# First cross attention of a two-layer Perceiver stack: query projection from half-precision parts

## The reference

```
Q = Sq @ Wq_w.T + Wq_b              # Sq = layernorm(x): 4 x 256 tokens, 256 -> 1024 (16 heads of 64)
K = Sk @ Wq_w.T + Wq_b              # Sk = Sv = context: 4 x 4096 rows
V = Sv @ Wq_w.T + Wq_b
qk = einsum('bqd,bkd->bqk', Q1, K1) / sqrt(64)
X1 = softmax(einsum('bqk,bkd->bqd', qk, V1), axis=-1)    # softmax over the 64 features of a head
x = x + X @ out_w.T + out_b
```

## Time and profile before

| | |
|---|---|
| Median of 3 runs | 1931.04 us (1930.85 to 1933.86) |
| Profiled execution | 1943.5 us, span 1941.8 us |
| Mean granted TensorE clock | 0.921 |
| PE busy | 1676.4 us, 86% of the span |
| DVE busy | 1316.1 us, 68% |
| ACT busy | 1083.6 us, 56% |
| Query projection, L1025 | 27.63 us, 64 records |

### The profile page before, as it was taken

The page is one execution under the profiler, slowest core; times in us unless marked ns, Lnnn a source line. Parts: engine busy times, 40 slices in busy tenths (PEclk is TensorE's granted clock), DMA queues, the critical chain, the costliest instruction groups (busy, mean ns, idle before and its releaser), DMA issues.

```text
span 1941.8 us, 34714 instructions
## 1 busy us (share of the span) xinstructions
PE 1676.4 (86%) x13900; PEld 913.9 (47%) x13900; DVE 1316.1 (68%) x2014; ACT 1083.6 (56%) x1942; POOL 276.1 (14%) x248
## 2 busy tenths in 40 slices
PE   6988868999798999846999999999999679886877
PEld 4556645666566888521333333333333433462252
DVE  4223343381276888659999999999991686427867
ACT  3312112888643888311999999999999106311620
POOL 3223001898320000300000000000000000000000
PEclk9989989999888999875999999999999779886978
DMA  8123110899723766266433533543400070118100
GB/s 321 66 87 94 32 44 20 279 282 298 228 96 107 240 237 200 69 100 93 84 60 74 99 65 63 91 84 60 83 25 2 19 98 3 44 35 106 39 1 22
DMA packets 144653, 196.62 MB, mean 101 GB/s; under 512 B 34454, under 2 KB 109864, under 8 KB 140232
## 3 DMA queue, kind: packets, MB, share of 16 engines
q1 hardware_dynamic: 142764, 190.07, 38.1%
q0 software_dynamic: 1728, 4.33, 0.7%
HBM read 143.04 MB, written 51.00 MB: 100 GB/s over the span
## 4 chain that ended last, share of the span: by engine, by line
PE 43%; DVE 41%; issue 5%; POOL 4%; DMA 3%; ACT 2%; SPq 1%; another core or an unknown queue 1%; DVEq 0%; ACTq 0%; POOLq 0%
DVE mx_part L2200 28%; PE bank L1192 5%; PE pair L1234 5%; DVE mx L2309 3%; POOL k_part L2541 2%; PE bank L1045 2%; PE bank L1336 2%; PE pair L1395 2%; PE bank L252 2%; PE pair L1160 2%; PE pair L1147 2%; PE bank L1089 2%; DMA xT<-x_slots 2%; POOL c_lo L2528 2%; PE pair L1551 2%
## 5 line engine op out<-in xcount | busy, mean ns | idle before, releaser
L1743 ACT ACTIVATE pexp_all<-bank 128x512 f32<-128x512 f32 x1024 | 551.9, 595 | 97.9 <-PE bank L1350 84.5
L2200 DVE TENSOR_REDUCE mx_part<-pair 128x2 f32<-128x1024 f32 x512 | 583.0, 1213 | 16.6 <-PE pair L1322 14.2
L1336 PE MATMUL bank<-pexp_all,vst 128*17 128x256 f32 x4096 | 321.4, 386 | 6.0 <-issue 6.0
L1322 PE MATMUL pair<-kst,qs 49*128 49x512 f16 x1024 | 210.0, 407 | 44.7 <-DVE mx_part L2200 28.0
L1350 PE MATMUL bank<-qs,kst 52*128 52x256 f16 x2048 | 203.2, 271 | 0.0
L1322 PEld LDWEIGHTS pair<-kst,qs 49*128 49x128 f16 x1024 | 50.4, 93 | 273.2 <-DVE mx_part L2200 215.0
L1350 PEld LDWEIGHTS bank<-qs,kst 52*128 52x128 f16 x2048 | 120.7, 95 | 57.0 <-ACT pexp_all L1743 18.4
L1760 ACT ACTIVATE pexp_all<-bank 128x512 f32<-128x512 f32 x128 | 67.6, 595 | 120.5 <-PE bank L1458 120.3
L1336 PEld LDWEIGHTS bank<-pexp_all,vst 128*17 128x17 f32 x4096 | 68.6, 95 | 114.7 <-issue 105.3
L1677 ACT ACTIVATE hid_f<-bank,b 128x256 f32<-128x256 f32 (+1 forms) x152 | 78.6, 519 | 51.1 <-PE bank L1192 36.0
L1234 PE MATMUL pair<-w_hi,hid_hi 128*128 128x256 f16 x368 | 101.1, 275 | 3.2 <-issue 1.8
(11 more groups left out here) (323 smaller groups left out, 3042.5 us busy)
## 6 DMA issues: line engine op xcount, KB each, us to landing
w_f<-in_w_all SPq DMA_DIRECT2D x34, 1024.0 KB, 6.2
kst<-k_scr SPq DMA_DIRECT2D x192, 128.0 KB
v_scr<-v_st SPq DMA_DIRECT2D x64, 272.0 KB, 3.3
vst<-v_scr SPq DMA_DIRECT2D x16, 1088.0 KB, 5.6
ctx_sb<-in_ctx SPq DMA_DIRECT2D x16, 1024.0 KB, 5.0
cT<-in_ctxT SPq DMA_DIRECT2D x32, 512.0 KB, 5.6
k_scr<-k_part SPq DMA_DIRECT2D x128, 128.0 KB, 3.6
x_slots<-zeros SPq DMA_DIRECT2D x1, 3840.0 KB, 21.1
```

The costliest lines, as they stand in the source:

```text
L1322: last = pe.matmul(pair[n % 2][:, e * 512:(e + 1) * 512], qs[g % NBK][rws, p, qt * P:(qt + 1) * P], kst[g % NBK][rws, p, kb * 512:(kb + 1) ...
L1336: last = pe.matmul(bank[3][32 * h:32 * h + HV, 0:S], vst[g % 2][:, c, h * HV:(h + 1) * HV], unit_exp[n % NUE][:, p * S:(p + 1) * S], start ...
L1743: act.activation(unit_exp[n % NUE], bank[SCORE_BANKS[n % 3]], ACT.Exp, scale=SCALE).then_inc(s_exp, 1)
L2200: dve.tensor_reduce(mx_part[:, :, 2 * p + qt, kb], pair[n % 2][:, :].rearrange("p (e k) -> p e k", e=2), X_AXIS, ALU.max).then_inc(s_mx, 1)
```

## The change

The projection L1025 is computed from half-precision parts. The scaled weights are split in high and low part, w0q_part, in the memory of tok; the turned tokens likewise, x0_part, in the memory of gw. The high part of the tokens is a second destination of the turn, so ACT copies each tile twice. Each single-precision matmul becomes three with half-precision operands. ACT makes the weights' high parts ahead of the turn, and waits for s_wa there. DVE makes the low parts, of the weights first and then of the tokens, behind the second Gram copy; the addition of the output bias to x moves behind them. PE waits for the count of low parts (s_q0p) in place of the turn. The eviction divides by W_SCALE.

```diff
+            w0q_part = tok[:, :, :].rearrange("p t d -> p (t d)").bitcast(F16).rearrange("p (i k n) -> p i k n", i=2, k=KT)
+            x0_part = gw[:, :, :].rearrange("p k n -> p (k n)").bitcast(F16).rearrange("p (i k n) -> p i k n", i=2, k=KT)
...
-        turn0 = Turn(u, [(xT, None, None)])
+        turn0 = Turn(u, [(xT, None, None), (x0_part[:, 0], None, None)])
...
             for half in range(2):
-                turned(pe, turn0, half)
+                pe.wait_ge(s_q0p, 4 + KT * (half + 1))
                 for m in range(W0 // P):
                     if job >= 2:
                         pe.wait_ge(s_q0e, job - 1)
                     for k in range(KT):
-                        last = pe.matmul(bank[2 + job % 2], w0q[:, k, m * P:(m + 1) * P],
-                                         xT[:, k, half * 512:(half + 1) * 512], start=(k == 0), stop=(k == KT - 1))
+                        for i, (w_, x_) in enumerate(((0, 0), (0, 1), (1, 0))):
+                            last = pe.matmul(bank[2 + job % 2], w0q_part[:, w_, k, m * P:(m + 1) * P],
+                                             x0_part[:, x_, k, half * 512:(half + 1) * 512],
+                                             start=(k == 0 and i == 0), stop=(k == KT - 1 and i == 2))
...
             act.wait_ge(s_start, 16 * N_START)
+            act.wait_ge(s_wa, 32)
+            for i in range(4):
+                k, ns = i // 2, slice(i % 2 * 512, (i % 2 + 1) * 512)
+                act.activation(w0q_part[:, 0, k, ns], w0q[:, k, ns], ACT.Copy, scale=W_SCALE).then_inc(s_q0h, 1)
             act_turn(act, turn0)
...
-                               bias=col("L0_xattn_Wq_b", m)).then_inc(s_q0e, 1)
+                               bias=col("L0_xattn_Wq_b", m), scale=1.0 / W_SCALE).then_inc(s_q0e, 1)
...
                 if b == 0:
                     dve.wait_ge(s_start, 16 * N_START)
-                    st.link(dve.tensor_tensor(x[:, :, :], x[:, :, :], per_tile_rows("L0_xattn_out_b"), ALU.add))
-                    st.settle()
...
                 dve.wait_ge(s_grame, 4 * (b + 1))
+                if b == 0:
+                    for i in range(4):
+                        k, ns = i // 2, slice(i % 2 * 512, (i % 2 + 1) * 512)
+                        dve.wait_ge(s_q0h, i + 1)
+                        dve.scalar_tensor_tensor(out=w0q_part[:, 1, k, ns], in0=w0q[:, k, ns], scalar=W_SCALE,
+                                                 in1=w0q_part[:, 0, k, ns], op0=ALU.mult, op1=ALU.subtract).then_inc(s_q0p, 1)
+                    for half in range(2):
+                        hs = slice(half * 512, (half + 1) * 512)
+                        for k in range(KT):
+                            dve.wait_ge(s_tev, turn0.ev + 2 * (2 * half + k + 1))
+                            dve.tensor_tensor(x0_part[:, 1, k, hs], xT[:, k, hs], x0_part[:, 0, k, hs], ALU.subtract)\
+                                .then_inc(s_q0p, 1)
+                    st.link(dve.tensor_tensor(x[:, :, :], x[:, :, :], per_tile_rows("L0_xattn_out_b"), ALU.add))
+                    st.settle()
```

More of the change, by code:

```diff
@@ L348, in build @@
         s_q0 = sem("q0_product")
+        s_q0h = sem("q0_weights_high")
+        s_q0p = sem("q0_operand_parts")
         s_q0e = sem("q0_copied")
```

## The result

| | before | after |
|---|---|---|
| Median of 5 runs | 1931.77 us (1930.85 to 1933.86) | 1913.98 us (1908.35 to 1919.23) |
| Profiled execution | 1943.5 us, span 1941.8 | 1914.0 us, span 1912.2 |
| Mean granted clock in it | 0.921 | 0.922 |
| Start of the gw products (L1842, after: L1864) | 67.10 | 60.94 |

The ratio is 0.9906, with an interval of 0.9888 to 0.9923: 17.8 us faster by the medians, where 7.1 was forecast.

The account below looks back on a forecast made before the run. The prediction took PE's matmul stream alone to bound the projection (L1025): 6.7 us from the shorter stream plus 0.4 from an earlier start made 7.1, so 1931.0 - 7.1 = 1923.9 us, range 1919 to 1930.

Parts of the forecast that it names:

- Length of the product: Projection L1025: 96 half-precision matmuls at 0.216 us take 20.9 us against 27.6, 6.7 us less.
- Second Gram copy and turn: Ahead of the projection: with the bias add moved, the copy starts at 31.85 and PE turns tokens 1.8 us earlier.
- ACT's conversions hidden behind w0o's arrival: Ahead of the turn: ACT's four weight conversions end at 32.1 to 32.7, hidden with 0.4 to 1.0 us slack.
- third rival: Weight w0o lands 1 to 3 us later, giving 1925 to 1927; chance within a shared 0.16.
- Start of the product: Projection starts at about 36.1 against 36.52 before, a gain taken as 0.4 us.
- Moved add hidden: On DVE behind the low parts: the bias add runs 38.1 to 40.4, hidden; in the open it would cost 2.2 us.
- Evictions: In the projection: ACT's eviction of 0.69 us fits within each 1.30 us job, with 0.5 us to spare.
- fourth rival: In the projection: half-precision matmuls overlap further, ACT's evictions become the bound at 11.0 us, time 1914; chance 0.01.
- All of it should shift together: Behind the projection: later stages keep their length, so the 7.1 us passes whole to the end.
- clock stretches: Behind the edit: a half-clock stretch comes or goes, 4 to 8 us either way; going away, 1915 to 1920, chance 0.09.
- Slower by the clock: Projection at 1.2 GHz takes 41 us, 14 more than before, so about 1944; slower by over 3.9 us has chance 0.06.

Follow-up runs that it names:

- e3: The kernel before with only the output bias addition to x moved behind the second Gram copy; 1926.91 us, ratio 0.9973.
- e7: The changed kernel with only the high-by-high product in the projection, both products with low parts left out; 1913.32 us, ratio 0.9905 to the kernel before.
- e5: The changed kernel again, unchanged, for the scatter of its median and a second profile; 1918.69 us, ratio 0.9935 to the kernel before.
- v1: The changed kernel with the product of Gram matrix and w0q also made from half-precision parts, split on DVE; 1940.75 us, ratio 0.994 to the kernel before.
- c4: The changed kernel with the Gram product from half-precision parts as well, ended after the first cross attention; median 279.34 us.

## Why the prediction was wrong, point by point

- **Length of the product:** forecast 20.9 us, measured 21.68, with 0.8 of it from half clock at its start, and 20.88 in the four other profiles of the changed code, at full clock; 0.216 us per matmul at full clock as in the earlier trace rows. The Trainium skill's sustained spacing of 131 ns (TensorE: Matmul & The Clock Gate, section Back-to-back issue gap) is not seen in this stream; its other formula, 216 ns, agrees with the row. Right.
- **Second Gram copy and turn:** 31.85 forecast, 32.00 measured. e3 gives 1.6 us for this part alone at a like clock in the turn (2.5 against the mean of before), where the prediction had 1.8. Right.
- **ACT's conversions hidden behind w0o's arrival:** end at 32.08, forecast 32.1 to 32.7. The third rival (w0o late) falls.
- **Start of the product:** 36.1 forecast, 36.31 measured. Right; but the start it was compared with, 36.52, was the exception. Five other executions of that code had 37.3 to 37.8, with half clock in the turn, so the gain at this step was nearer 1.3 than 0.4 in most executions.
- **Moved add hidden:** yes, 38.17 to 40.45, wanted at 60.94.
- **Evictions:** ACT idles 0.61 us in each job. The fourth rival falls, though the number that it gave, 1914, is the measured one, by luck. A right number doesn't make a mechanism right: its sign, PE waiting for ACT, is in e7 alone.
- **All of it should shift together:** this is the step that failed. 7.1 us is what the edit saves (7.0 at a like clock, 67.10 to about 60.1), and the prediction took that as the sum for the whole kernel, with the clock stretches at nothing in the sum, as luck in both directions, and a gain from them at 0.09. The runs show three terms more, all on the side of the gain: 1 us from half clock in the turn, which the base has in five of six profiles and the changed code in one of five; 1.3 us from the long stretch, five of six against three of five; and 3.7 us behind the first block, whose length isn't fixed as was assumed "for the rest of the span" but has three levels. The base was one profile, which was the exception in the turn. It had the long stretch at 131.8 in plain sight, with 8.6 us of lost work, and from one profile it couldn't be known whether that was rule or luck. Another 4.6 us of the 17.8 are likely the draw of five executions. What sets how often the stretches come, and which stage makes the levels, stays open.
- **Slower by the clock:** the projection ran at 0.96 mean clock; this rival falls.

The Trainium skill puts such falls of the clock down to PE waiting for DMA between short stages (TensorE: Matmul & The Clock Gate, section HAM oscillation — how this bites in real kernels). In e5's stretch the DMA share is 0.00 and PE is busy 16.14 of 17.1 us, and in the 11.9 us before it, with a DMA share of 0.76, PE was busy for 11.13, as it was in the execution in which the clock stayed full. So no such wait stands ahead of this fall. In v1 PE did wait 6.2 us ahead of its half clock, for DVE and not for a DMA.

No version ran that beats the changed kernel with the whole computation in it: v1 lost what its shorter stream had won in the split on DVE beside POOL. A v1 with that split in another place or on another engine wasn't tried.

## What to carry to other kernels

Splitting a single-precision product into three half-precision ones saves a quarter of its stream when the parts can be made under idle engines; work out which engine makes each part and when its operand lands, and the local saving comes out within a microsecond. Check beside what each of these instructions will run: one that takes 0.4 us alone can take 4.0 beside another engine. Stretches behind the edit, at half clock or not, needn't keep their length when they are reached earlier, so profile the base several times before you call one of its stretches fixed, and compare executions at a like mean clock. A difference of two profiles is no measure: here it was 29.6 us where the medians gave 13 to 18 and the start behind the edited stage 8.

## What was not expected of the hardware

- PE can be granted 1.2 GHz for 17.1 us while busy for 16.1 of them; the same code in another execution gets 3.4 us of it.
- DVE's subtraction of 128x257 took 4.04 us in each of four cases beside POOL's subtraction of ctx_lo (v1, c4), and 0.43 in each of eight without it; the conversion ahead of it 1.37 and 0.3.
- Time follows the mean granted clock from execution to execution: 289.1 us at 0.929 and 285.2 at 0.954 in the first block of before.
- Chips differ: the same kernel took 1930 us on two of them, 1947 and 1952 on two others, more than this change brings.
